# Expert 0's first 128 slots: the first product made in rows, ahead of the main tiles

## The reference

```python
x = x + jnp.tanh(g_xattn[0]) * _L0_xattn_ref(_layernorm(x, axis=-1), ctx_2048)
x = x + jnp.tanh(g_ffn[0]) * _L0_ffn_ref(_layernorm(x, axis=-1), Wg, w1, w2)
# _L0_ffn_ref, per token: the two best of 8 experts, 640 slots for each expert
probs = jax.nn.softmax(xr @ Wg, axis=-1)
gate_vals, expert_idx = jax.lax.top_k(probs, K)
pos = jnp.sum((jnp.cumsum(oh, axis=0) - 1) * oh, axis=1)   # slot: how many tokens chose this expert before
kept = pos < C                                              # C = 640
h = jax.nn.relu(jnp.einsum('ecd,edf->ecf', dispatched, w1))   # 512 -> 2048
expert_out = jnp.einsum('ecf,efd->ecd', h, w2)                # 2048 -> 512
out = jnp.einsum('ks,ksm->sm', combine_weights, rerouted)
```

## Time and profile before

| what | us |
|---|---|
| median of 3 runs (lowest, highest) | 872.28 (871.55, 872.7) |
| the profiled execution | 866.91 |
| its span, first to last instruction | 865.0 |
| TensorE busy | 808.1 |
| VectorE busy | 600.4 |
| ScalarE busy | 357.7 |
| GpSimd busy | 226.0 |

### The profile page before, as it was taken

One profiled execution on the slowest core, in us unless ns is written; L12 is line 12 of the kernel. 1 busy time (PEld: TensorE's weight loads), 2 busy tenths in 40 slices (PEclk: granted clock), 3 DMA queues, 4 the chain that ended last, 5 costly groups with the idle time before them and its releaser, 6 DMA issues.

```text
span 865.0 us, 12186 instructions
## 1 busy us (share of the span) xinstructions
PE 808.1 (93%) x4297; PEld 387.3 (45%) x4298; DVE 600.4 (69%) x958; ACT 357.7 (41%) x586; POOL 226.0 (26%) x219
## 2 busy tenths in 40 slices
PE   0598995899999999999999999999999999999995
PEld 0444665444444444444444444444444444444442
DVE  6999998376767885778576767766775678565430
ACT  4897994342514252434241424241425142504310
POOL 3132131773431044005301440043003310332010
PEclk9999998699999999999999999999999999999999
DMA  8703334975657274539541845264636372612000
GB/s 303 283 1 139 138 139 177 228 194 98 118 164 242 97 166 160 194 97 194 181 177 63 169 176 176 97 146 149 227 97 138 135 251 97 129 43 61 1 27 23
DMA packets 79289, 123.17 MB, mean 142 GB/s; under 512 B 43390, under 2 KB 43406, under 8 KB 75168
## 3 DMA queue, kind: packets, MB, share of 16 engines
q1 hardware_dynamic: 68032, 93.33, 35.5%
q0 software_dynamic: 10944, 29.51, 12.6%
q10 hardware_dynamic: 288, 0.00, 0.0%
HBM read 96.53 MB, written 18.95 MB: 133 GB/s over the span
## 4 chain that ended last, share of the span: by engine, by line
PE 87%; DVE 5%; DMA 2%; SPq 2%; ACT 2%; issue 1%; POOL 0%; ACTq 0%; POOLq 0%; DVEq 0%
PE mm L857 39%; PE mm L787 38%; PE mm L582 4%; DMA w_stage<-in_L_ffn_w 2%; PE mm L766 2%; PE mm L827 2%; SPq L328 1%; SPq L327 1%; DVE region L1255 1%; DVE region L1259 1%; PE mm L571 1%; SPq L332 0%; DMA region<-x_split,row_next 0%; PE marks_ps L623 0%; DVE region L1400 0%
## 5 line engine op out<-in xcount | busy, mean ns | idle before, releaser
L857 PE MATMUL mm<-region,w_split 128*128 128x512 f16 x1536 | 335.8, 381 | 1.5 <-ACT region L1009 1.5
L787 PE MATMUL mm<-region 128*128 128x512 f16 x1536 | 335.8, 379 | 0.0
L857 PEld LDWEIGHTS mm<-region,w_split 128*128 128x128 f16 x1536 | 150.9, 98 | 185.0 <-issue 5.6
L787 PEld LDWEIGHTS mm<-region 128*128 128x128 f16 x1536 | 148.8, 98 | 181.2 <-issue 4.2
L1130 ACT ACTIVATE region<-mm 128x512 f16<-128x512 f32 x128 | 76.4, 597 | 310.4 <-PE mm L857 310.4
L1562 DVE SCALAR_TENSOR_TENSOR region<-mm,region 128x512 f16<-128x512 f32 x128 | 88.6, 692 | 114.2 <-ACT region L1130 114.2
L506 POOL DMA_INDIRECT out<-region,back_now x40 | 65.1, 1627 | 168.3 <-DVE region L1575 143.1
L1565 DVE SCALAR_TENSOR_TENSOR region<-w_stage,w_scale,region 128x512 f16<-128x512 f32 x128 | 96.2, 752 | 0.0
L1133 ACT ACTIVATE region<-w_stage,w_scale 128x512 f16<-128x512 f32 x128 | 91.2, 712 | 0.0
L1361 DVE SCALAR_TENSOR_TENSOR w_split<-w_stage,w_scale,w_split 128x2048 f16<-128x2048 f32 x32 | 74.0, 2349 | 3.4 <-ACT w_split L893 1.8
L1348 DVE TENSOR_REDUCE top<-w_stage 128x1 f32<-128x512 f32 x112 | 76.0, 679 | 0.0
(11 more groups left out here) (189 smaller groups left out, 578.4 us busy)
## 6 DMA issues: line engine op xcount, KB each, us to landing
w_stage<-in_L_ffn_w SPq DMA_DIRECT2D x64, 1024.0 KB, 5.4
region<-in_x SPq DMA_DIRECT2D x4, 1024.0 KB, 13.2
x_split<-region SPq DMA_DIRECT2D x8, 512.0 KB, 2.9
out<-region SPq DMA_DIRECT2D x4, 1024.0 KB, 5.3
w_stage<-in_ctx SPq DMA_DIRECT2D x2, 1024.0 KB, 11.6
region<-in_ctx SPq DMA_DIRECT2D x2, 1024.0 KB, 14.9
region<-x_split,row_next POOLq DMA_INDIRECT x40, 4.3
region<-out,row_next POOLq DMA_INDIRECT x40, 4.5
```

The lines of the kernel that those rows point to most:

```text
L787: mm = pe.matmul(mm2[s % 2][:, :], hidden[:, hh, f, s * P:(s + 1) * P], w2_split[:, wh, f, :], start=(f == 0 and hh + wh == 0), stop=(f == ...
L857: mm = pe.matmul(products(f), w1_split[:, wh, k, f * P:(f + 1) * P], xT[:, xh * KD + k, 0:WIDE], start=(k == 0 and wh + xh == 0), stop=(k ...
```

## The change

Expert 0's first 128 slots take tokens of the first three batches only (12 tiles); were there fewer than 128, the slots that lack stay empty and later tokens move up (`lack`). So their rows can be found before the last batch is chosen: VectorE makes their 128 columns of the one-hots apart (`early_onehots`), TensorE finds the rows (`find_early`), and GpSimd gathers them with one transfer (`gather_early`). TensorE turns that slot tile and makes its whole first product in rows: the 128 slots stand and 512 hidden columns of the weights move, in four quarters of twelve products (`early_product`). ScalarE and VectorE write the high and low halves (`early_high`, `early_low`), TensorE turns them back in four pieces of eight between main tiles of expert 0 (`turn_early`), and ScalarE puts them where the main tiles' results go (`keep_early`). Expert 0's main tiles then move 384 columns. The order on every engine changes around this. TensorE's and ScalarE's loops are cut elsewhere (the second product of one expert and the first of the next form a turn), and VectorE's and SyncE's first expert stands ahead of the loop.

The core of the diff, in the order SyncE, GpSimd, TensorE, ScalarE, VectorE:

```diff
+SOON = 3 * MT
+QUADS = F // WIDE
...
+        early_xT = cut(0, 2, F16).rearrange("p (j c) -> p j c", j=2 * KD)
+        early_x = cut(2, 2, F16)
+        early_rows = cut(64, 8, F16).rearrange("p (h f) -> p h f", h=2)
+        early_banks = [mm1[1][:, 0, :], mm1[1][:, 1, :], mm2[1][:, :], mm1[1][:, 0, :]]
+        def columns_from(e):
+            return P if isinstance(e, int) and e == 0 else 0
+        def early_piece(j):
+            return j % 2, slice((j // 2) * 2 * KD, (j // 2 + 1) * 2 * KD)
...
-            for b in range(B):
+            for b in range(B - 1):
                 store_split(b, 0)
                 store_split(b, 1)
                 store_rows(b)
+            store_rows(B - 1)
...
+            load_w1_part(1, 0, 0)
+            store_split(B - 1, 0)
+            store_split(B - 1, 1)
             sp.wait_ge(x_got[FULL - 1], 16)
             alone(sp, q["sp_passed"])
-            load_w1_part(1, 0, 0)
+            sp.wait_ge(q["w1_lo"], 2)
+            sp.dma_start(w1_stage[:, 1, :], w1_t[1, :, 1, :]).then_inc(w1_in[1], 16)
...
-                for s in range(NS):
+                for s in range(1 if first else 0, NS):
                     pool.indirect_dma_start(
                         x_slots[:, s, :], None, xsplit,
...
+            def gather_early():
+                pool.wait_ge(q["early_row"], 1)
+                pool.wait_ge(q["split_out"], 32 * (B - 1))
+                pool.wait_ge(q["rows_out"], 16 * B)
+                pool.indirect_dma_start(
+                    early_x, None, xsplit[0:SOON * P, :],
+                    bass.IndirectOffsetOnAxis(ap=row_next[:, 0:1], axis=0)).then_inc(x_got[0], 16)
...
-            pool.wait_ge(q["split_out"], 32 * B)
+            gather_early()
+            pool.wait_ge(q["split_late"], 32)
             gather_x(0, first=True)
             pool.wait_ge(q["zeros_in"], 16)
             pool.wait_ge(q["notes_ready"], 1)
-            pool.wait_ge(q["rows_out"], 16 * B)
             gather_acc()
...
+            def find_early():
+                for i in range(SOON):
+                    pe.wait_ge(q["early_onehot"], i + 1)
+                    if i == 0:
+                        pe.wait_ge(q["sums_read"], 2)
+                    mm = pe.matmul(found_ps[:, 0, 0:1], first_onehot(i)[:, 0:P], marks[:, i, 0:1],
+                                   start=(i == 0), stop=(i == SOON - 1), skip_group_check=True)
+                mm.then_inc(q["early_found"], 1)
             def find_rows(i0, i1):
+                pe.wait_ge(q["early_row"], 1)
                 for i in range(i0, i1):
                     pe.wait_ge(q["onehot_ready"], i + 1)
-                    for s in range(NS):
+                    for s in range(1, NS):
...
+            def early_product(n, ks):
+                if 0 in ks:
+                    if n == 0:
+                        pe.wait_ge(xT_in[0], 16)
+                        pe.wait_ge(q["prod_read"], NT)
+                        pe.wait_ge(q["w1_hi"], KD)
+                        pe.wait_ge(q["w1_lo"], KD)
+                    if n == QUADS - 1:
+                        pe.wait_ge(q["early_lo"], 1)
+                for k in ks:
+                    for wh, xh in ((0, 0), (0, 1), (1, 0)):
+                        mm = pe.matmul(early_banks[n], early_xT[:, xh * KD + k, :],
+                                       w1_split[:, wh, k, n * WIDE:(n + 1) * WIDE],
+                                       start=(k == 0 and wh + xh == 0), stop=(k == KD - 1 and wh == 1),
+                                       skip_group_check=True)
+                if KD - 1 in ks:
+                    mm.then_inc(q["early_done"], 1)
+            def turn_early(j):
+                h, fs = early_piece(j)
+                if j < 2:
+                    pe.wait_ge(xT_in[FULL - 2 + j], 16)
+                    pe.wait_ge(q["early_lo"], QUADS)
+                else:
+                    pe.wait_ge(q["early_kept"], j - 1)
+                for t in range(2 * KD):
+                    f = fs.start + t
+                    mm = pe.transpose(xT_banks[j % 2][:, t, :], early_rows[:, h, f * P:(f + 1) * P], ident16[:, :])
+                mm.then_inc(q["early_back"], 1)
...
-            router(2, [2])
+            router(2, [2, 3])
             turn_norm(3, [0])
-            router(2, [3])
             turn_norm(3, [1])
             router(3, [0])
+            place(1)
             turn_norm(3, [2])
             router(3, [1])
-            place(1)
             turn_norm(3, [3])
+            find_early()
             router(3, [2, 3])
-            find_rows(0, 7)
+            find_rows(0, SOON)
+            turn_slots(0, xT_banks[0])
+            early_product(0, (0, 1))
             place(2)
-            find_rows(7, 16)
-            turn_slots(0, xT_banks[0])
+            early_product(0, (2, 3))
+            find_rows(SOON, NT)
+            early_product(1, range(KD))
             turn_slots(1, xT_banks[1])
             turn_slots(2, xT_banks[0])
+            early_product(2, range(KD))
             turn_slots(3, xT_banks[1])
+            early_product(3, range(KD))
...
+            EARLY_TURNS = (2, 3, 5, 6)
-            def expert(e, last):
+            def first(e):
+                at = columns_from(e)
...
+                    if at > 0 and f in EARLY_TURNS:
+                        turn_early(EARLY_TURNS.index(f))
...
-                            mm = pe.matmul(products(f), w1_split[:, wh, k, f * P:(f + 1) * P], xT[:, xh * KD + k, 0:WIDE],
+                            mm = pe.matmul(products(f)[:, at:WIDE], w1_split[:, wh, k, f * P:(f + 1) * P],
+                                           xT[:, xh * KD + k, at:WIDE],
...
+            first(0)
+            pe.wait_ge(q["early_kept"], QUADS)
             with nc.tensor.Fori(0, E - 1) as e:
-                expert(e, False)
-            expert(E - 1, True)
+                rest_of(e, False)
+                first(e + 1)
+            rest_of(E - 1, True)
...
-            normalise(3, [0, 1])
+            normalise(3, [0])
+            keep_logits(1)
+            normalise(3, [1])
             copy_norm(3, [0])
-            keep_logits(1)
...
             keep_logits(2)
+            first_columns(0)
             exponents()
-            first_columns(0)
+            early_high(0)
             first_columns(1)
+            early_high(1)
             first_columns(2)
             first_columns(3)
+            early_high(2)
+            early_high(3)
...
+                if g == 1:
+                    prep.step(V.tensor_scalar(lack[:, 0:1], place_ps[:, NT, 0:1], -1.0, float(P), ALU.mult, ALU.add))
+                    prep.step(V.tensor_scalar(lack[:, 0:1], lack[:, 0:1], 0.0, None, ALU.max))
+                    prep.step(V.tensor_scalar(lack[:, 1:2], lack[:, 0:1], 1.0, None, ALU.add))
+                base = lack[:, 1:2] if g == 2 else 1.0
...
+            def early_row():
+                dve.wait_ge(q["early_found"], 1)
+                V.tensor_scalar(row_next[:, 0:1], found_ps[:, 0, 0:1], -1.0, 0.0, ALU.add, ALU.max).then_inc(q["early_row"], 1)
...
             norm_scale(3)
+            norm_scale(4)
+            choose(1)
+            early_onehots(0, 8)
+            first_scale(1)
+            first_places(1)
+            early_onehots(8, SOON)
             first_onehots(0, 2)
-            norm_scale(4)
-            first_scale(1)
-            first_onehots(2, 6)
-            choose(1)
+            early_row()
             low_rows(3, 0)
-            first_onehots(6, 7)
-            first_places(1)
-            first_onehots(7, 12)
+            first_onehots(2, 8)
             low_rows(3, 1)
             choose(2)
+            first_onehots(8, SOON)
+            first_places(2)
+            first_onehots(SOON, NT)
             powers()
-            first_places(2)
-            first_onehots(12, 16)
             first_rows()
             places()
             list_loads()
             gates()
+            early_low(0)
+            early_low(1)
             notes_of_rows()
+            early_low(2)
+            early_low(3)
```

More of the change, by code:

```diff
@@ L199, in build @@
         loads = sb("loads", [P, E], I32)
+        lack = sb("lack", [P, 2], F32)
         row_a = sb("row_a", [P, NT], F32)
@@ L220, in build @@
         is_small = sb("is_small", [P, E], F32)
+        room_used = sb("room_used", [P, E], F32)
         top1 = sb("top1", [P, NF], F32)
@@ L400, in weights @@
                 turn_slots(e + 1)
-            with nc.sync.Fori(0, E - 2) as e:
+            weights(0, True)
+            load_w1_part(2, 0, 1)
+            with nc.sync.Fori(1, E - 2) as e:
                 weights(e)
@@ L1120, in _, with first_half @@
             keep_logits(2)
+            first_columns(0)
             exponents()
-            first_columns(0)
+            early_high(0)
             first_columns(1)
+            early_high(1)
             first_columns(2)
             first_columns(3)
-            def expert(e, last):
+            early_high(2)
```

(24 more changed lines are left out.)

57 lines of the change are left out of this document (38 added, 19 removed).

## The result

| what | before, us | after, us |
|---|---|---|
| median (lowest to highest, runs) | 872.49 (871.55 to 873.20, 4) | 884.66 (880.23 to 887.47, 4) |
| profiled execution (span) | 866.91 (865.0) | 880.23 (878.6) |

After takes 1.0122 times as long, 95% interval 1.0090 to 1.0155: 12.2 us more by the medians, 13.3 between the profiled executions. 881.2 us had been predicted, 874 to 887.

A forecast was written before the change was run, and what follows sets the result against it. Two chains, TensorE's and GpSimd's notes, meet at `turn_rows`, GpSimd's 2.0 us earlier. A start 6.6 us later plus 2.3 us of slow clock gives +8.9 us on the 872.28 us median: 881.2 us, range 874 to 887.

The forecast's parts named there:

- Part 2: From last choice to slot rows: early work delays the last placing, so `row_next` ends at 155.7, 7.9 us later.
- the low and the high clock: TensorE's early product: a 512-column product costs 0.44 us at the low clock, 0.218 at the high one.
- The early gather: Forecast in time for 147.5; the rival has it land late, at 149.6, +2.1 us, 883.3 us, chance 0.12.
- Part 3: Slot rows to notes: `acc` fetched at 167.4 (+12.2 us), notes end 9.6 us later, `turn_rows` starts 6.6 us later.
- the two paced waits: GpSimd's two waits for main tiles among the notes, 1.3 us each beyond the usual 0.3, would fall away.
- The landing: The last note's time from start to landing on GpSimd's chain: 5.3 us taken instead of 6.3.
- No gap ahead of `turn_rows`: Sign of a wrong forecast; the right one was a TensorE gap of 6 to 11 us ending with `low_rest`.
- 226 to 231: Sign of a right forecast: the time at which `turn_rows` starts on TensorE, forecast at 228.5.
- Part 4: Expert 0's narrower tiles take 33 us, ending at 201.3; TensorE reaches `turn_rows` at 219.7 and stands about 9 us.
- 2.3 us for a slow clock behind it: Loss to TensorE's lowered clock after the gap ahead of `turn_rows`: 2.3 us, bounds 1.2 to 3.0.
- Faster: Rival: TensorE's chain ends last, the notes come as early as before, tiles gain 2.2 us: 870.1 us, chance 0.07.
- VectorE paces the tiles: Rival: VectorE's three operations a tile take as long as 384 columns, so tiles shrink less; counted in the forecast's time.

The follow-up runs named there:

- e1_place: The changed kernel with the last group's place and all slot rows ahead of the first turn and early product on TensorE: 882.28 us, ratio 1.0103.
- e3_both: The changed kernel with the last group's place ahead of the early product and the notes ahead of the early low halves: 873.39 us, ratio 1.0002.
- e7_notes_late: The changed kernel with last placing and notes moved ahead of the early work, and every note waiting for all 16 main tiles: 897.05 us.
- e5_before: The kernel before, unchanged, run once more for a second profile: 875.07 us, span 873.1.
- e6_acc_late: The changed kernel with last placing and notes moved ahead of the early work, and the acc fetches behind the 32 notes: 876.80 us, ratio 1.0028.
- e4: The kernel before with only the loops of TensorE, ScalarE and VectorE cut as in the changed kernel: 872.38 us, ratio 0.9989.
- e8: The kernel before with the five acc fetches moved behind the 32 notes: 878.09 us, ratio 1.0046.
- e9_before_notes_late: The kernel before with every note waiting until all 16 of expert 0's first-product tiles are done: 907.08 us.
- e12: The kernel before with the loops recut and expert 0's `low_rest(0)` ahead of VectorE's waits for acc, maximum and entries: 872.94 us, ratio 0.9968.

## Why the prediction was right, and where it was off

**The deciding step held.** Part 2 put the slot rows at 155.7: measured 156.47, +8.7 where 7.9 was said. The 0.8 us came in ahead of it: a 128-column one-hot took 0.17 (eight in 1.39) where 0.12 was guessed, and the one-hots ended at 147.99 instead of 147.2. From there to the slot rows it took 8.5 us, just the sum of part 2, but not by its reason: the 0.8 was taken off for a clock that rises on the way, and the granted clock stayed at 0.50 (150 to 156, both halves of the product); what was saved lay in the short steps between. No run shows the 2.6 us in that sum for six products, an estimate of mine; the two halves took 2.74 and 2.72 us (150.36 and 153.15). What part 2 calls the low and the high clock are, in the trace of before, granted clocks of 0.50 (159.05 to 164.39, tile 0) and 1.00 (166 to 203). The early gather came in time: the turns at 148.18 waited for no gather, so that rival falls. Part 3 had `acc` fetched at 167.4: 167.23. That close a hit is luck as well: from slot rows to `acc` it took 10.8 us instead of 11.7, and that made up for the 0.8. e1 to e3 confirm the cause: with both orders undone the ratio goes from 1.0122 to 1.0002.

**The notes' end was mis-sized.** Part 3 had the notes end 9.6 us later, since the two paced waits would fall away; they ended 15.6 later. Part 3 forecast 40.3 us from the first note to the last (42.9 before, less 2.6); it took 46.5. The tiles did not run ahead: GpSimd stood 1.12 and 1.89 us among the notes for tiles that were themselves late. It also stood 2.71 us ahead of the note at 186.46, which waits for three tiles only (`note_after(8)`), and these were done by 177.3: a hole of GpSimd's own. The rest is notes that took longer. In e3_both it was 46.5 us again (163.97 to 210.42). The landing came out at -1.6 (4.70 us against 6.29) where -1.0 was taken; the 1.0, for a weight load no longer beside it, was my estimate, and no run shows that a load has this effect. In e7_notes_late the last note was in 2.64 us after its start (238.17 to 240.81, DMA share 0.02), under the 3.3 to 8.5 of the earlier trace rows; in after it took 4.70 at a share of 0.59 and in e3_both 7.62 (210.42 to 218.04) at 0.64, within them.

**The gap ahead of `turn_rows` did not appear.** "No gap ahead of `turn_rows`" was one of the prediction's own signs of being wrong, and `turn_rows` at 233.76 lies outside the 226 to 231 that it gave as a sign of being right. Part 4 had the tiles at 168 to 201.3 and TensorE then idle for 9 us. They ran from 170.8 to 214.8, 44.0 us for 33, and the gap was 0.35 us. e7_notes_late shows the 33.0 to be right for tiles alone; what part 4 missed are the holes of TensorE and ScalarE among GpSimd's transfers (up to 1.09 and 7.46 us here). The trace of before had no such hole, so it could not show this; e5_before does. The gap was thus spread through the tiles rather than standing at their end. The 2.3 us for a slow clock behind it were not paid there either: the granted clock fell to 0.50 in 185 to 190, inside the tiles, after the few products of 180 to 185, and stood at 1.00 from 233.8 to 243, behind `turn_rows`.

**The sum.** +6.6 and +2.3 were forecast at `turn_rows` and behind it; +11.8 and +1.3 were measured, 13.1 against 8.9. By the medians, which have the holes on both sides, it is 12.2. The sign and its cause were right; the size was 3.3 us short. That it was no further off is partly luck. The notes' end (15.6 for 9.6) and the tiles (44.0 for 33) were both too small, but in the profiled execution the two chains ended within 0.35 us of each other, so that only one of them counted; and the 1.3 us behind `turn_rows` were holes, not the slow clock that the forecast had there.

**The rivals.** Faster would have needed slot rows within 0.4 us of before; even e3_both, which nearly has this (gathers at 150.13 against 148.65), only comes out equal: the tiles' gain goes into holes, and the notes' chain ends last by 3.36 us. That VectorE paces the tiles is not seen: in 180 to 185 it is busy for 0.00 us and waits for ScalarE. For e6_acc_late and e3_both I was wrong in the same way twice: I counted on the tiles' gain, and another chain (the late `acc` rows there, the notes here) took it.

## What to carry to other kernels

Work that fills an idle stretch must not stand, in an engine's program, ahead of what the next chain waits for: in after VectorE stood 5.34 us for the last placing behind half an early product, in e1_place GpSimd 9.79 us for the notes behind `early_low(1)`, and the early product cost nothing that could be measured (ratio 1.0002) once both went ahead of it. When a chain ends last at one step, ask also whether that step needs the chain at all: `low_rest(0)` only stood behind the notes in VectorE's program, and moving it ahead brought 0.9% in after and 0.5% in e3_both, where the narrower tiles had brought nothing that could be measured; the 0.2% in the kernel without the early product lie within the noise. And take a second profile when the profiled execution lies well under the median: here the first one lacked a stop of ScalarE, 1.85 to 4.88 us, that the five later ones without the early product had ahead of the tiles (e4, e5, e8, e9, e12).

## What the runs showed of the hardware

In these runs TensorE and ScalarE nearly stopped at times while GpSimd issued indirect transfers one after another, without any semaphore being late that the trace shows. In e7_notes_late TensorE was busy for 4.12, 3.65 and 2.93 us in three windows of 10, at a DMA share of 0.02 and 1 GB/s. The holes began about 12 us behind the first note there (198.17; first hole before 210.97), and the last of them ended at 243.23, 4 us behind the last note. In after ScalarE stood 7.46 us (to 185.70) among the notes. In e5_before and e9_before_notes_late it stood like this (4.88 us to 163.62, 4.09 to 162.53) ahead of the tiles, in the former beside the last `acc` fetches and the first two notes (158.16 to 164.26), in the latter beside the last `acc` fetches and for 1.3 us behind them, with no note written yet. It does not always happen: in e6_acc_late the tiles lost only 2.7 us beside the notes. Late instructions are a guess that no run here settles.
